# Experts: VectorE instead of TensorE transposes the gathered rows, one unit ahead, in 32x32 blocks

## What is computed

```python
xn = _layernorm(x)                                   # x: 8 x 1024 x 256
x  = x + attn(xn, ...) + ffn(xn, gate_w, Wg, Wu, Wd)  # 16 heads of 16; 8 experts, 256 -> 512 -> 256

# ffn: each expert takes its 256 best rows of each of the 8 batches
affinity = jax.nn.softmax(jnp.einsum('bsd,de->bse', x, gate_w), axis=-1)
gating, index = jax.lax.top_k(jnp.transpose(affinity, (0, 2, 1)), K)     # K = 256
x_sel = x[b_idx, index]
g = jnp.einsum('bekd,edi->beki', x_sel, Wg)
u = jnp.einsum('bekd,edi->beki', x_sel, Wu)
h = jax.nn.silu(g) * u
out = jnp.einsum('beki,eid->bekd', h, Wd)
x_out = jnp.zeros_like(x).at[b_idx, index].add(out * gating[..., None])
```

## Time and profile before

| | us |
|---|---|
| median of 3 runs (1703.66 to 1705.21) | 1703.79 |
| the profiled execution | 1702.51 |
| its span, first to last instruction | 1700.7 |
| first gate_up of unit 0 to the end of the span | 574.3 |
| TensorE, VectorE, ScalarE, GpSimd busy | 1659.8, 1076.0, 1247.7, 522.7 |

### The profile page before, as it was taken

The page is one execution under the profiler, slowest core; times in us unless marked ns, Lnnn a source line. Parts: engine busy times, 40 slices in busy tenths (PEclk is TensorE's granted clock), DMA queues, the critical chain, the costliest instruction groups (busy, mean ns, idle before and its releaser), DMA issues.

```text
span 1700.7 us, 28137 instructions
## 1 busy us (share of the span) xinstructions
PE 1659.8 (98%) x10616; PEld 921.9 (54%) x10616; DVE 1076.0 (63%) x2350; ACT 1247.7 (73%) x1544; POOL 522.7 (31%) x480
## 2 busy tenths in 40 slices
PE   6799999999999999999999999999999999999997
PEld 5234344334433433433434433358888888888886
DVE  8874586487477467568558648866455555455543
ACT  5698988998898899899898899964444444444443
POOL 3121111101211111112112100036666565666653
PEclk9799999999999999999999999999999999999998
DMA  5644745764574475465474466345444444434332
GB/s 183 163 102 119 151 98 115 176 129 107 149 169 110 121 159 143 112 145 138 119 161 103 116 139 142 61 146 105 102 94 63 96 78 84 97 65 94 65 57 33
DMA packets 113984, 196.02 MB, mean 115 GB/s; under 512 B 20896, under 2 KB 59680, under 8 KB 113696
## 3 DMA queue, kind: packets, MB, share of 16 engines
q1 hardware_dynamic: 83696, 143.01, 36.6%
q0 software_dynamic: 29040, 49.83, 14.9%
q10 hardware_dynamic: 1088, 1.05, 0.2%
HBM read 117.27 MB, written 76.55 MB: 114 GB/s over the span
## 4 chain that ended last, share of the span: by engine, by line
PE 93%; DVE 4%; DMA 1%; POOL 1%; issue 1%; ACT 0%; POOLq 0%; DVEq 0%; ACTq 0%
PE o_ps L1036 28%; PE score L1118 21%; PE score L1022 20%; PE side L905 5%; PE score L1129 3%; PE side L915 3%; PE side L946 3%; PE o_ps L1129 2%; PE score L1131 2%; PE side L1129 2%; PE score L1105 2%; PE side L889 1%; PE o_ps L1131 1%; PE side L1131 1%; DMA probs<-in_wk_t 0%
## 5 line engine op out<-in xcount | busy, mean ns | idle before, releaser
L807 ACT ACTIVATE probs<-score 128x1024 f32<-128x1024 f32 x1024 | 967.8, 1063 | 103.4 <-PE score L1022 101.1
L1036 PE MATMUL o_ps<-probs,v_ones 128*32 128x512 f32 x4096 | 523.8, 604 | 0.8 <-DVE o_sb L1516 0.6
L1022 PE MATMUL score<-q_stack,k_stack 50*128 50x512 f32 x2048 | 395.6, 458 | 5.1 <-issue 4.5
L1022 PEld LDWEIGHTS score<-q_stack,k_stack 50*128 50x128 f32 x2048 | 164.0, 185 | 353.1 <-ACT probs L807 310.3
L705 POOL DMA_INDIRECT out<-probs,rot x128 | 212.3, 1658 | 189.1 <-DVE probs L1481 159.8
L786 ACT ACTIVATE probs<-score 128x512 f32<-128x512 f32 x128 | 76.7, 599 | 186.8 <-PE score L1118 186.8
L1467 DVE TENSOR_TENSOR probs<-score,probs 128x512 f32<-128x512 f32 x128 | 88.6, 692 | 181.0 <-PE score L1118 176.6
L1036 PEld LDWEIGHTS o_ps<-probs,v_ones 128*32 128x32 f32 x4096 | 92.2, 108 | 200.0 <-issue 139.2
L683 POOL TENSOR_TENSOR square<-qk 128x512 bf16<-128x512 f32 x56 | 77.2, 1407 | 387.6 <-DVE qk L1320 387.6
L694 POOL DMA_INDIRECT qk<-xn_rows,rot x128 | 135.5, 1059 | 38.3 <-issue 29.3
L1118 PE MATMUL score<-k_stack,zn_hi 128*128 128x512 f32 x512 | 140.1, 390 | 0.0
(11 more groups left out here) (274 smaller groups left out, 2382.7 us busy)
## 6 DMA issues: line engine op xcount, KB each, us to landing
q_parts<-parts SPq DMA_DIRECT2D x16, 1024.0 KB, 4.3
k_parts<-parts SPq DMA_DIRECT2D x16, 1024.0 KB, 7.4
q_stack<-q_parts SPq DMA_DIRECT2D x62, 256.0 KB, 7.1
k_stack<-k_parts SPq DMA_DIRECT2D x62, 256.0 KB, 8.8
q_stack<-q_parts SPq DMA_DIRECT2D x66, 128.0 KB, 7.4
k_stack<-k_parts SPq DMA_DIRECT2D x66, 128.0 KB, 8.1
o_sums<-o_sb SPq DMA_DIRECT2D x256, 32.0 KB
num<-o_sums SPq DMA_DIRECT2D x32, 256.0 KB
```

Source lines behind the costliest of these rows:

```text
L807: act.activation(probs[probs_of(b, s)][:, 2 * i:2 * i + 2, :], score[ring_of(b, p)][:, :, :], ACT.Exp, scale=SCALE).then_inc(exp_done, 1)
L1022: last = pe.matmul(score[ring_of(b, p)][:, w, :], k_stack[par][rows, i, kt * P:(kt + 1) * P], q_stack[par][rows, i, qh * HALF:(qh + 1) * H ...
L1036: last = pe.matmul(o_ps[j * KEYS_W:(j + 1) * KEYS_W, :], v_ones[par][:, kt, j, :], probs[probs_of(b, s)][:, j, :], start=kt == 0, stop=kt ...
```

## The change

The eight transposes on TensorE stay for unit 0 alone (`turn_first`). For every later unit VectorE transposes the gathered rows itself, 32x32 block by block, into `x_turned` (the space of the attention part's cosine table, tile `cos_sb`): `turn_rows(unit, a)` issues four instructions, each reads 32 partitions (rows a) and 256 elements and writes to 32 other partitions. Four calls (a = 0 to 3) make a unit, 16 instructions. They stand a unit ahead in VectorE's list: a = 0 of unit + 2 ahead of unit's four L1481, a = 1 ahead of the first `h` of unit + 1, a = 2 and 3 behind its first and second `h`. Casting and subtracting `x_hi` and `x_lo` is then one instruction each of 1024 columns instead of two of 512, and ScalarE's also waits until gate_up of the unit before is over (`up_full`). `low_weights` moves ahead of `turn_rows(unit + 2, 0)` and of the L1481. On TensorE down(unit) follows gate_up(unit) at once; it uses the two banks `xt_ps` for t = 2 and 3, and does blocks f = 0, 1 of all four tiles, then f = 2 of all four, then f = 3. The output projection's quarters move from units 0 and 1 (behind down) to units 1 and 2 (between gate_up and down). GpSimd's gather waits for VectorE's turning instead of TensorE's.

```diff
@@ rows_ps
-        return (d_ps[0], d_ps[1], g_ps[(FC - 1) % 2], u_ps[(FC - 1) % 2])[t]
+        return (d_ps[0], d_ps[1], xt_ps[0], xt_ps[1])[t]
...
-    END_BANKS = {("wo", q): (q // 2, q % 2) for q in range(QUARTERS)}
+    END_BANKS = {("wo", q): (q // 2 + 1, q % 2 + 2) for q in range(QUARTERS)}
@@ ScalarE
         def turned(unit):
...
+            else:
+                act.wait_ge(rows_turned, unit)
+                act.wait_ge(up_full, FC * unit)
+                act.copy(x_hi[:, :, :], x_turned).then_inc(x_high, 1)
@@ TensorE
-            for t in range(2):
-                part(t, (FC - 2,))
-            for t in range(2):
-                part(t, (FC - 1,)).then_inc(down_full, 1)
-            for t in range(2, ST):
-                part(t, range(FC)).then_inc(down_full, 1)
+            if unit + 1 < E * UNITS:
+                for t in range(ST):
+                    part(t, (FC - 2,))
+                for t in range(ST):
+                    part(t, (FC - 1,)).then_inc(down_full, 1)
...
             gate_up(unit)
-            if unit + 1 < E * UNITS:
-                turn(unit + 1)
@@ VectorE
+        def turn_rows(unit, a):
+            if unit >= E * UNITS:
+                return
+            if a == 0:
+                dve.wait_ge(gathered[unit % 2], ST * DMA * (unit // 2 + 1))
+                dve.wait_ge(x_split, splits_of(unit - 1))
+            rows = slice(a * BLOCK, (a + 1) * BLOCK)
+            from_rows = xs[unit % 2][rows, :, :].rearrange("p t (c q n) -> p q c t n", c=DC, n=BLOCK)
+            to_cols = x_turned.rearrange("p c (t a k) -> p a c t k", t=ST, k=BLOCK)
+            for q in range(BLOCKS):
+                last = dve.transpose(to_cols[q * BLOCK:(q + 1) * BLOCK, a, :, :, :], from_rows[:, q, :, :, :])
+            if a == BLOCKS - 1:
+                last.then_inc(rows_turned, 1)
...
             e, bp, par = unit // UNITS, unit % UNITS, unit % 2
+            turn_rows(unit + 1, 1)
             for f in range(FC):
...
                 dve.tensor_tensor(h[f % 2], u_ps[f % 2], silu[f % 2], ALU.mult).then_inc(h_done, 1)
+                if f + 2 < BLOCKS:
+                    turn_rows(unit + 1, f + 2)
                 if f > 0:
                     low(unit, f - 1)
...
+            if bp < WEIGHTS and e + 1 < E:
+                low_weights(e + 1, bp)
+            turn_rows(unit + 2, 0)
             for t in range(ST):
                 dve.wait_ge(y_begun, ST * unit + t + 1)
...
-            if bp < WEIGHTS and e + 1 < E:
-                low_weights(e + 1, bp)
```

More of the change, by code:

```diff
@@ L24 @@
 LANE = 64
+BLOCK = 32
+BLOCKS = P // BLOCK
 LANES = P // LANE
@@ L689, in gather @@
             need(pool, scattered[bp], ST * DMA * e)
-            need(pool, xt_full, DC * (unit - 1))
+            if unit == 2:
+                pool.wait_ge(xt_full, DC)
+            elif unit > 2:
+                pool.wait_ge(rows_turned, unit - 2)
             pool.tensor_copy(rows_now[bp], rows_flat[:, e * COLS + bp * ST:e * COLS + (bp + 1) * ST]).then_inc(rows_set, 1)
@@ L773, in turned @@
         def turned(unit):
-            for c in range(DC):
-                act.wait_ge(xt_full, DC * unit + c + 1)
-                act.copy(x_hi[:, c, :], xt_ps[c]).then_inc(x_high, 1)
+            if unit == 0:
+                for c in range(DC):
+                    act.wait_ge(xt_full, c + 1)
+                    act.copy(x_hi[:, c, :], xt_ps[c]).then_inc(x_high, 1)
+            else:
+                act.wait_ge(rows_turned, unit)
+                act.wait_ge(up_full, FC * unit)
+                act.copy(x_hi[:, :, :], x_turned).then_inc(x_high, 1)
         def high(unit, f):
@@ L1096, in _, with turn_first @@
         attend(NB - 1, None, NB - 2)
-        def turn(unit):
-            pe.wait_ge(gathered[unit % 2], ST * DMA * (unit // 2 + 1))
+        def turn_first():
+            pe.wait_ge(gathered[0], ST * DMA)
             for c in range(DC):
-                need(pe, x_split, DC * unit + c - 1)
-                if unit in (2, 3):
-                    pe.wait_ge(side_free, end_jobs.done(("wo", 2 * (unit - 2) + c)))
                 for t in range(ST):
-                    last = pe.transpose(xt_ps[c][:, t * P:(t + 1) * P], xs[unit % 2][:, t, c * P:(c + 1) * P], ident_sb[:, :])
+                    last = pe.transpose(xt_ps[c][:, t * P:(t + 1) * P], xs[0][:, t, c * P:(c + 1) * P], ident_sb[:, :])
                 last.then_inc(xt_full, 1)
@@ L1153, in _ @@
             gate_up(unit)
-            if unit + 1 < E * UNITS:
-                turn(unit + 1)
+            for job in END_JOBS:
+                if END_BANKS[job][0] == unit:
+                    pe.wait_ge(y_scaled, ST * (unit - 1) + END_BANKS[job][1] + 1)
+                    run_job(end_jobs, job, None, NB - 1, rows_ps(END_BANKS[job][1]))
             if unit == 0:
@@ L1452, in turned @@
         def turned(unit):
-            for c in range(DC):
-                dve.wait_ge(x_high, DC * unit + c + 1)
-                dve.tensor_tensor(x_lo[:, c, :], xt_ps[c], x_hi[:, c, :], ALU.subtract).then_inc(x_split, 1)
+            if unit == 0:
+                for c in range(DC):
+                    dve.wait_ge(x_high, c + 1)
+                    dve.tensor_tensor(x_lo[:, c, :], xt_ps[c], x_hi[:, c, :], ALU.subtract).then_inc(x_split, 1)
+            else:
+                dve.wait_ge(x_high, splits_of(unit))
+                dve.tensor_tensor(x_lo[:, :, :], x_turned, x_hi[:, :, :], ALU.subtract).then_inc(x_split, 1)
+        def turn_rows(unit, a):
[11 more added lines that the diff above has]
+                last.then_inc(rows_turned, 1)
         def low(unit, f):
@@ L1467, in expert_unit @@
                 dve.tensor_tensor(h[f % 2], u_ps[f % 2], silu[f % 2], ALU.mult).then_inc(h_done, 1)
+                if f + 2 < BLOCKS:
+                    turn_rows(unit + 1, f + 2)
                 if f > 0:
                     low(unit, f - 1)
+            for job in END_JOBS:
+                if END_BANKS[job][0] == unit:
+                    take(end_jobs, job, None, NB - 1, rows_ps(END_BANKS[job][1]))
             low(unit, FC - 1)
@@ L1483, in expert_unit @@
                                          ALU.mult, ALU.add).then_inc(y_scaled, 1)
-            for job in END_JOBS:
-                if END_BANKS[job][0] == unit:
-                    take(end_jobs, job, None, NB - 1, xt_ps[END_BANKS[job][1]])
-            if bp < WEIGHTS and e + 1 < E:
-                low_weights(e + 1, bp)
         def take(jobs, job, n, d, bank):
```

23 lines of the change are left out of this document (14 added, 9 removed).

## The result

| | before | after |
|---|---|---|
| median (lowest to highest), us | 1703.72 (1703.63 to 1705.21), 4 runs | 1792.60 (1791.21 to 1793.88), 4 runs |
| ratio, 95% interval | | 1.0519, 1.0501 to 1.0538 |
| profiled execution, its span | 1702.51, 1700.7 | 1791.21, 1789.4 |
| granted clock, mean | 0.991 | 0.972 |

The change makes the kernel slower by 5.2%, 88.9 us. The forecast was 1786 us, within 1738 to 1808.

A forecast was written before the change was run, and what follows sets the result against it. TensorE, busy 98% of the span, was taken to bound the kernel. +7 (first three units), +82.7 (19 after a weight split), -7.7 (nine others) and +0.6 (end) make +82.6: 1786 us on the median, range 1738 to 1808.

The forecast's parts named there:

- TensorE's gain: Expert part: without eight transposes (0.79 us) a unit falls from 17.35 to about 16.5 us; 27 us if VectorE's work were free.
- t = 0.47: VectorE: time for each new 32-partition, 256-column transpose, 0.47 us with its gap; sixteen make 7.5 us a unit.
- The appointment: Weight-split units: `low_weights` waits for ScalarE's cast, transposes and scalings queue behind it; TensorE waits 3.6 us for the first `h`.
- The second wait, 0.6: Later in a weight-split unit TensorE waits 0.6 us more for VectorE; this goes if the clock falls.
- The clock: Weight-split units: the 3.6 us wait halves TensorE's clock for about 3.3 us, losing 1.65 us of work; unit 21.7 us.
- The 19 units: Units from the fourth on that follow a weight split: 4.35 us longer each, 82.7 us together.
- The first three units, +7: Units 0 to 2, with output projection and its splitting: from 60.4 to 66 to 69 us, +7.
- "about 3" of the 5.07 us of splitting: Units 1 and 2: of VectorE's splitting ahead of `low_weights`, about 3 us fall where it would wait for the cast anyway.
- The nine others, -7.7: Units from the fourth on that follow no weight split: 0.86 us shorter each, -7.7 us together.
- The clock held: Rival: TensorE keeps full clock despite the waits in weight-split units; 1766 us, 17%.
- Cheap and dear transposes: Two rivals on VectorE: transposes at 0.34 us, mostly around 1760 us, 20%; at 0.60 or held up by GpSimd, 1826 us, 6%.
- GpSimd's loop: Rival: the round of scatter, gather, transposes and scaling binds at 17.5 us a unit, VectorE's late start does not; 1708 us, 4%.

The follow-up runs named there:

- gathers early: The changed kernel with GpSimd's gathers three units ahead instead of two: alone 1795.2 us, ratio 1.0542; also added to other edited kernels.
- the run with 128 partitions: The changed kernel with four transposes of 128 partitions for sixteen of 32 (rows in a wrong layout, only time read): 1690.4 us, ratio 0.9930.
- The filled wait: The changed kernel with eight added matmuls on TensorE ahead of block 2 in the 21 gate_ups behind a weight split: 1780.3 us, ratio 1.0459.
- the cast first: The changed kernel with ScalarE's cast of the next expert's weights moved ahead of its four scalings: 1721.3 us, ratio 1.0114.
- `low_weights` last: The changed kernel with `low_weights` moved back behind VectorE's four scalings: 1726.1 us, ratio 1.0139.

## Why the prediction was right, point by point

- **What bounds, and TensorE's gain.** "A unit becomes about 16.5 us": 16.47 wherever nothing waits, in every kernel with the gathers early. Right.
- **One transpose, t = 0.47.** 0.436 long, and four take 1.78, so 0.447 apart. The estimated length of 433 to 459 ns was right at its lower end, and there is no overlap but a pause of about 0.01, not 0.04. The Trainium skill, page "VectorE: DVE Perf Modes", section "Two Vector instructions with no wait between them", fits both ways: 0.447 for 0.436 where the 32-partition group changes, and 0.36 for 0.44 in the run with 128 partitions.
- **The appointment.** Cast ready at 1.76 us after the start of gate_up (1.65 said), `low_weights`, transposes, scalings, transposes, first `h` ready at 8.9 (9.09). The order of events was as written, in all 19 units. The wait was 3.27 instead of 3.6: half of the difference is 8 x 0.023 from t, the other half is that the wait begins 0.18 us later, when the last matmul has left the engine. What the appointment costs was shown by three runs: move the cast, 71 us come back; move the subtraction, 66; shorten what stands behind it, 102.
- **The second wait, 0.6.** 0.4, and only where the clock held, as said. Such a unit is 20.72 (20.7 said).
- **The clock.** Mis-sized. It was to fall in every one of the 19 and make each 1.0 us longer, 19 us in all. It fell in 13: eleven became 0.7 to 1.0 longer, two 2.1, together 13.6. The filled wait took just this away. In the run with only the gathers early it fell in 16.
- **The 19 units.** 77.8 us instead of 82.7, the sum of the points above.
- **The first three units, +7.** The term that was mis-sized, and the step that failed: +14.7. TensorE waits in them for 4.10, 5.23 and 3.84 us, 13.2 us against 1.9 of idle time before. Three times eight transposes less take 2.6 us off. The rest, about 6 us, is an estimate of what the lower clock (0.89 over the three) costs its own work: 61.85 us busy against 58.44 less 2.6 before. The row is that of units 0 to 2 of after; the second line is VectorE ahead of unit 0's first product.

```profile
1126.64:1201.65 75.01, 61.85 (x292) 51.49 (x289) 60.30 (x115) 23.71 (x41) 25.26 (x22) 0.89 0.45 114
1132.13 3.58 DVE L1484 STREAM_TRANSPOSE cos_sb<-qk 32x256 f32<-32x256 f32 x8 [4.66 <-DMA qk<-xn_rows,rot]
```

  Two things were wrong. Unit 0 was put at no wait at all, but VectorE waited 4.66 us for the second unit's rows and then made eight transposes: `turn_rows(1, 0)` and `turn_rows(1, 1)` have no unit before them to lie in. And units 1 and 2 were not added up by the prediction's own terms: 3.6 of wait and 1.65 of clock in each, the 2 us of each splitting that stick out, less 0.86 three times, make about 12 and not 7. That "about 3" of the 5.07 us of splitting "lie where it would wait for the cast anyway" came out: the two waits are 2.0 and 0.6 us longer than 3.27. Since the splits end after the cast, an earlier cast gains nothing here (waits of 5.22 and 3.84, and 75.4 in all, with the cast first).
- **The nine others, -7.7.** -4.7. The prediction worked out a round of 17.5 us over GpSimd and said that it eats part of it. Four of the nine were 17.22 to 17.27, released by the gather; with the gathers a unit earlier all nine are 16.47.
- **Rivals.** The clock held in 6 of 19 units only. Cheap and dear transposes are out by the 0.447. GpSimd's loop was no rival but the next in line: it is what binds as soon as the appointment is repaired (16 us), and VectorE's load is the likely next (17.14 against 16.47, 19 times, 12.7 us).

The prediction's errors partly cancel, and that 1792.6 lies so near 1786 is in part luck: -4.9 in the 19 units, +7.7 in the first three, +3.0 in the nine, +0.3 at the ends, +6.1 in the profiled execution.

## What to carry to other kernels

Work that is moved to a half-empty engine goes into an ordered list: look for the instruction in it that waits for a fixed event (here a cast which another engine does last), and add up what now stands between it and the next result that the busy engine needs; that sum, not the share of busy time, decided here: 89 us lost where 27 were to be gained. Then look for the loops just longer than the new unit, since each repair uncovers the next: cast (71 us), gather (16), and then VectorE's own 17.1 us against 16.5. And a split that stands early may be what starts a transfer: before moving one, see what its end releases.

## What the runs showed of the hardware

- A transpose of 32-bit elements on VectorE in 32x32 blocks, SBUF to SBUF, 256 columns, takes 0.436 us on 32 partitions and 0.42 to 0.44 on 128.
- Two-input work on GpSimd and on VectorE, both in SBUF, did not run side by side: a 0.69 us subtraction of VectorE's took 2.43 us and 4.07 us beside a 2.9 us one of GpSimd's, while VectorE's transposes and a product that reads PSUM kept their 1.78 to 1.80 and 0.69 us beside it. On GpSimd the subtraction took 2.99 us against 1.22.
- With 19 equal waits of 3.27 us in one execution of after, the clock fell with 13 of them (in five it was at half when the wait ended, in eight it fell within 2 us behind it) and not with the other six; in units 3 to 30 of the kernel with the waits filled down to 1.46 us, and one of 2.23, it never did. Waits of 2.35 and 2.00 us in the run with `low_weights` last did bring it down. What tells the two kinds apart stays open. Windows of 1 us behind the waits that end at 1271.5 and 1292.96 (the clock is the last number but two):

```profile
1272.00:1273.00 1.00, 1.00 (x4) 0.71 (x4) 0.97 (x3) 0.13 (x1) 1.00 (x1) 0.50 0.98 102
...
1294.00:1295.00 1.00, 1.00 (x6) 0.81 (x5) 0.97 (x3) 0.33 (x1) 0.82 (x1) 1.00 0.69 106
```
